# Routed experts in tiles of 128 tokens with the tokens stationary, in a pipeline of slots, instead of jobs of 256 rows

## The reference

```python
x = x + cross_attention(layernorm(x), ctx)       # 16 heads, causal mask
n = layernorm(x)                                 # 3584 x 512
probs = softmax(n @ gate_w.T)                    # 8 experts, the best 2 are taken
h1 = einsum("nc,efc->enf", n, expert_fc1)        # F_MOE = 352
h2 = einsum("nc,efc->enf", n, expert_fc2)
out_e = einsum("enf,ecf->enc", silu(h1) * h2, expert_proj)
y = einsum("ne,enc->nc", combine, out_e)         # combine: the 2 chosen probabilities
shared = (silu(n @ shared_fc1.T) * (n @ shared_fc2.T)) @ shared_proj.T   # F_SHARED = 1408
x = x + y + sigmoid(n @ shared_gate_w.T) * shared
```

## Time and profile before

| | us |
|---|---|
| median of 3 runs | 1603.74 |
| lowest and highest | 1602.83, 1603.98 |
| profiled execution, its own time | 1605.36 |
| its span, first to last instruction | 1603.6 |
| PE busy in the span | 1562.4 (97%) |
| DVE, ACT, POOL busy | 871.7 (54%), 633.1 (39%), 552.1 (34%) |

### The profile page before, as it was taken

The page is one execution under the profiler, slowest core; times in us unless marked ns, Lnnn a source line. Parts: engine busy times, 40 slices in busy tenths (PEclk is TensorE's granted clock), DMA queues, the critical chain, the costliest instruction groups (busy, mean ns, idle before and its releaser), DMA issues.

```text
span 1603.6 us, 32042 instructions
## 1 busy us (share of the span) xinstructions
PE 1562.4 (97%) x11388; PEld 1333.7 (83%) x11388; DVE 871.7 (54%) x1685; ACT 633.1 (39%) x1970; POOL 552.1 (34%) x507
## 2 busy tenths in 40 slices
PE   6999999999889999999999999999999999999998
PEld 5888888888678899999999999788788888888886
DVE  5667777776655666666666666554433232232322
ACT  5877777777823333333333333332112111121111
POOL 3233445544342365555555555121100101000010
PEclk9999999999999999999999999999999999999999
DMA  5133445443365366666666666354402103030110
GB/s 184 54 94 94 96 89 97 92 93 70 98 180 123 133 253 237 236 245 241 237 245 236 243 224 243 141 197 164 132 27 74 58 0 107 24 105 26 60 46 27
DMA packets 85684, 213.53 MB, mean 133 GB/s; under 512 B 38208, under 2 KB 39232, under 8 KB 80864
## 3 DMA queue, kind: packets, MB, share of 16 engines
q1 hardware_dynamic: 73424, 179.20, 34.7%
q0 software_dynamic: 12176, 33.20, 6.2%
HBM read 163.35 MB, written 49.02 MB: 132 GB/s over the span
## 4 chain that ended last, share of the span: by engine, by line
PE 89%; DVE 3%; issue 3%; ACT 2%; POOL 2%; DMA 1%; SPq 0%; DVEq 0%; POOLq 0%; ACTq 0%
PE psum L665 56%; PE psum L974 11%; PE psum L919 9%; PE psum L763 2%; PE psum L890 2%; PE psum L754 2%; PE psum L852 2%; ACT probs L1073 1%; PE psum L782 1%; PE psum L791 1%; PE psum L814 1%; PE psum L771 1%; POOL xn L1285 1%; DMA wj_raw<-in_wq 1%; PE psum L678 1%
## 5 line engine op out<-in xcount | busy, mean ns | idle before, releaser
L665 PE MATMUL psum<-gT_hi,wj_hi 128*128 128x256 f32 (+1 forms) x840 | 239.2, 285 | 0.0
L665 PE MATMUL psum<-gT_lo,wj_hi 128*128 128x256 f32 (+1 forms) x840 | 236.7, 282 | 0.0
L665 PE MATMUL psum<-gT_hi,wj_lo 128*128 128x256 f32 (+1 forms) x840 | 236.0, 281 | 0.0
L1360 POOL DMA_INDIRECT routed<-expert_out_dram,slot_b x56 | 56.2, 1004 | 487.6 <-DVE slot_b L1757 335.6
L665 PE MATMUL psum<-nT_hi,ws_hi 128*128 128x512 f32 x528 | 209.5, 397 | 6.1 <-DVE nT_lo L1709 6.1
L1775 DVE TENSOR_TENSOR h_s<-psum,silu_s 128x512 f32<-128x512 f32 x66 | 45.6, 691 | 306.2 <-PE psum L665 306.2
L665 PE MATMUL psum<-nT_hi,ws_lo 128*128 128x512 f32 x528 | 210.7, 399 | 0.0
L665 PE MATMUL psum<-nT_lo,ws_hi 128*128 128x512 f32 x528 | 210.0, 398 | 0.0
L1322 POOL TENSOR_SCALAR wj_hi<-wj_raw 128x2816 fp32r<-128x2816 f32 x68 | 136.5, 2024 | 151.9 <-PE psum L919 128.9
L1073 ACT ACTIVATE probs<-psum,minus_max 112x112 f32<-112x112 f32 x512 | 176.2, 429 | 2.5 <-DVE minus_max L1455 2.5
L1699 DVE TENSOR_TENSOR wj_lo<-wj_raw,wj_hi 128x2816 fp32r<-128x2816 f32 x70 | 169.2, 2417 | 0.8 <-ACT wj_hi L1165 0.7
(11 more groups left out here) (219 smaller groups left out, 3578.4 us busy)
## 6 DMA issues: line engine op xcount, KB each, us to landing
wj_raw<-in_w_experts SPq DMA_DIRECT2D x35, 2176.0 KB, 8.4
expert_out_dram<-y_c SPq DMA_DIRECT2D x35, 512.0 KB, 2.7
wj_raw<-in_w_shared SPq DMA_DIRECT2D x22, 768.0 KB, 5.6
base<-x_dram SPq DMA_DIRECT2D x8, 1024.0 KB, 5.9
x_in<-in_x SPq DMA_DIRECT2D x32, 224.0 KB, 4.5
x_res<-in_x SPq DMA_DIRECT2D x32, 224.0 KB, 3.9
x_dram<-x SPq DMA_DIRECT2D x32, 224.0 KB, 3.0
normed_dram<-xn SPq DMA_DIRECT2D x32, 224.0 KB, 4.9
```

What stands on the lines that cost most here:

```text
L665: mm = pe.matmul(out_ap, u, v, start=(n == 0), stop=(n == last))
L1360: pool.indirect_dma_start(out=routed[:, b % 2, c, :], out_offset=None, in_=expert_out_dram, in_offset=bass.IndirectOffsetOnAxis(ap=slot_b[ ...
```

## The change

The expert stage works on 63 tiles of 128 token rows. The first 56 positions of the table hold 28 pairs (two tiles of one expert, one load of weights), the last 7 hold odd tiles of one expert each, with a load of their own. They are worked in 7 rounds of 9: four pairs and then one odd tile. So there are 35 weight loads as before.

Tokens are now stationary also in the hidden products: 128 tokens x 128 channels stay, and all 352 features of one matrix move. h1, h2 and h then have tokens on the partitions, so h must be transposed before the projection (`rows_up`: 3 transposes, at columns 0, 128 and 224; the weight rows of the overlapping 32 features are zero in the third block). The projection has 3 x 3 products of 512 columns for a tile.

Each engine runs slots: PE in slot k does the hidden products of tile k, the transposes of h of k-1, the transposes of the tokens of k+2, the projection of k-2. There is one PSUM bank for each of h1, h2, hT, xT and y, one `h_c`, three buffers of xg, gT, hT and y_c, and three of the weights (pairs alternate between two, odd tiles have the third). Weights are loaded and split in two parts (`fc` 2816 columns, `pj` 1536) with semaphores of their own, spread over the slots by `splits`. ACT alone empties y. The first tile's weights are no longer loaded ahead with expert 0 fixed, but after the table, which is worked out across 128 partitions and brought to one row by two products on PE. In the last round the first shared chunk and the first tokens of the third stage are split in slots 8 and 7.

The table, the order of the weight splits, and the first weights' load:

```diff
-        NJOBS = (2 * NTOK + EXPERTS * (JOB - 1)) // JOB
+        TILES = (2 * NTOK + EXPERTS * (P - 1)) // P
+        ROUNDS = TILES // ROUND
+        PAIRS, SINGLES = 4 * ROUNDS, ROUNDS
...
+        def splits(q, k, fc, pj):
+            if k == 0:
+                fc(q, 1)
+            elif k == 1:
+                pj(q, 0)
...
+            elif k == 3:
+                pj(q, 1)
+                pj(q, 4)
...
                 if g == NG and j == 2:
-                    wait_emptied(sp, NG, 1, "proj")
-                    sp.dma_start(wj_raws[0][:, :], w_experts[0]).then_inc(wjraw_loaded[0], 16)
...
+            sp.wait_ge(S["table_ready"], 1)
+            wait_emptied(sp, NG, 1, "proj")
+            load_fc(0, 0)
+            load_pj(0, 0)
```

PE, beside the last shared chunks, and in the stage:

```diff
             for c in TAIL_CHUNKS:
-                chunk0(c)
+                hidden0(c)
+                if c == TAIL_CHUNKS[0]:
+                    pe.wait_ge(S["table_step"], TABLE_STEPS - 1)
+                    for i in range(2):
+                        mm = pe.matmul(psum[0:1, 6, i * TILES:(i + 1) * TILES], tile_cols[0:TILES, i:i + 1], ident[0:TILES, 0:TILES], start=True, stop=True)
+                    mm.then_inc(S["table_step"], 1)
+                project0(c - 1)
...
+            def hidden(q, k):
+                w, b = weights_of(k), k % 3
+                if first_of(k):
+                    pe.wait_ge(S["wc_split"], fc_nth(q, 4 if k == 8 else k // 2))
+                pe.wait_ge(S["gT_split"], tile(q, k) + 1)
+                for half, (to, emptied_h, made) in enumerate(((H1_BANK, "silu_made", "h1_done"), (H2_BANK, "h_made", "h2_done"))):
...
+                    for c in range(KC):
+                        cols = slice((half * KC + c) * FE, (half * KC + c + 1) * FE)
+                        pairs.append(((gT_hi[b][:, c, :], gT_lo[b][:, c, :]), (wj_hi[w][:, cols], wj_lo[w][:, cols])))
+                    product(bank(to, P, FE), pairs).then_inc(S[made], 1)
+            def rows_up(q, k):
+                pe.wait_ge(S["h_made"], tile(q, k) + 1)
...
+                for i, at in enumerate(F_AT):
+                    mm = pe.transpose(psum[:, HT_BANK, i * P:(i + 1) * P], h_c[:, at:at + P], ident[:, :])
...
+            def slot(q, k):
+                if is_tile(q, k):
+                    hidden(q, k)
+                if is_tile(q, k - 1):
+                    rows_up(q, k - 1)
+                if is_tile(q, k + 2):
+                    tokens(q, k + 2)
+                if is_tile(q, k - 2):
+                    project(q, k - 2)
```

ACT's slot, and what it does before the last shared chunk:

```diff
+            def slot(q, k):
+                if is_tile(q, k - 3):
+                    y_out(q, k - 3)
+                if is_tile(q, k):
+                    silu_of(q, k)
+                if is_tile(q, k - 1):
+                    rows_hi(q, k - 1)
+                if is_tile(q, k + 2):
+                    tokens_hi(q, k + 2)
+                if is_round(q, ROUNDS - 1):
+                    if k == 7:
+                        split_nT_hi(1)
+                    if k == 8:
+                        split_ws_hi(0)
...
+            for c in TAIL_CHUNKS:
+                if c == SC - 1:
+                    act.wait_ge(w_fc_loaded[0], 16)
+                    act.activation(wj_hi[0][:, FC_COLS], wj_raws[0][:, FC_COLS], ACT.Copy).then_inc(S["wc_hi_made"], 1)
                 chunk0(c)
```

DVE's product of silu(h1) and h2:

```diff
+            def h_of(q, k):
+                if not (isinstance(q, int) and tile(q, k) == 0):
+                    dve.wait_ge(S["hT_done"], tile(q, k))
+                dve.wait_ge(S["silu_made"], tile(q, k) + 1)
+                dve.wait_ge(S["h2_done"], tile(q, k) + 1)
+                dve.tensor_tensor(h_c[:, :], bank(H2_BANK, P, FE), silu_c[:, :], ALU.mult).then_inc(S["h_made"], 1)
```

More of the change, by code:

```diff
@@ L184, in build_program @@
         chosen = sa("chosen", [SEQ, TB + 1, EXPERTS])
[L185 to L190, removed]
+        tile_no_i, tile_no = sa("tile_no_i", [P, 2], I32), sa("tile_no", [P, 2])
+        expert_no, expert_at = sa("expert_no", [P, EXPERTS]), sa("expert_at", [P, EXPERTS])
+        steps_f = sa("steps_f", [P, EXPERTS, 2, STEPS])
+        over = sa("over", [P, EXPERTS, 2, STEPS])
+        counts, ends = sa("counts", [P, EXPERTS, 2]), sa("ends", [P, EXPERTS, 2])
+        jb = {n: sa("jb_" + n, [P, EXPERTS]) for n in
+              ("total", "begin", "begin2", "end2", "at", "late", "odd_at", "from_pair", "from_odd", "pair", "odd", "tile")}
+        spilled = sa("spilled", [P, 1])
+        tile_cols = sa("tile_cols", [P, 2])
         v_sb = sa("v_sb", [SEQ, 2, C])
@@ L342, in jobs @@
-        def jobs(eng, body):
-            pairs = (NJOBS - 2 - 3) // 2
-            for n in range(3):
-                body(n, n % 2)
-            with eng.Fori(0, pairs) as i:
-                body(2 * i + 3, 1)
-                body(2 * i + 4, 0)
-            for n in range(3 + 2 * pairs, NJOBS):
-                body(n, n % 2)
-        def last_job(n):
-            return isinstance(n, int) and n == NJOBS - 1
-        def is_job(n):
-            return not isinstance(n, int) or n < NJOBS
-        def times(k, n, p):
-            return (k // 2) * (n - p) + k
@@ L625, in _, with body @@
+            def body(q):
+                for k in range(ROUND):
+                    slot(q, k)
+            rounds(sp, body)
+            for k in range(ROUND, ROUND + 3):
+                store_y(ROUNDS - 1, k - 3)
+            for b in range(3):
+                sp.wait_ge(y_stored[b], 16 * TILES // 3)
             sp.wait_ge(S["phase_c_done"], 4)
@@ L893, in hidden @@
-            def hidden(n, p, i):
-                at, rows = F_CHUNKS[i]
-                for c, stage in enumerate(("h1", "h2")):
-                    b = take_c(n, stage, i)
-                    pairs = []
-                    for k in range(KC):
-                        cols = slice(c * KC * FE + k * FE + at, c * KC * FE + k * FE + at + rows)
-                        pairs.append(((wj_hi[p][:, cols], wj_lo[p][:, cols]), (gT_hi[:, k, :], gT_lo[:, k, :])))
-                    product(bank(b, rows, JOB), pairs).then_inc(filled_c[b], 1)
@@ L940, in _ @@
             pe.wait_ge(h2_emptied, SC)
-            tokens(0, 0, range(KC))
+            tokens(0, 0)
             project0(SC - 1)
-            jobs(pe, job_body)
-            pe.wait_ge(S["y_filled"], NJOBS)
+            tokens(0, 1)
+            rounds(pe, body)
+            for k in range(ROUND, ROUND + 2):
+                slot(ROUNDS - 1, k)
+            pe.wait_ge(S["y_done"], TILES)
             pe.sem_inc(S["phase_c_done"], 1)
@@ L1132, in split_ws_hi, with y_out @@
+            def y_out(q, k):
+                b, nth = turn(q, k)
+                if not (isinstance(q, int) and tile(q, k) < 3):
+                    act.wait_ge(y_stored[b], 16 * (nth - 1))
+                act.wait_ge(S["y_done"], tile(q, k) + 1)
+                act.activation(y_c[b][:, :], bank(Y_BANK), ACT.Copy).then_inc(S["y_emptied"], 1)
             def split_ws_hi(i):
@@ L1171, in _ @@
-            act.wait_ge(S["y_emptied"], JT * NJOBS)
+            for k in range(-2, 0):
+                slot(0, k)
+            rounds(act, body)
+            for k in range(ROUND, ROUND + 3):
+                slot(ROUNDS - 1, k)
+            act.wait_ge(S["y_emptied"], TILES)
             act.sem_inc(S["phase_c_done"], 1)
```

652 lines of the change are left out of this document (372 added, 280 removed).

## The result

The changed kernel takes 1554.62 us (median of 4, 1553.38 to 1559.25), the one before 1603.86 beside it: ratio 0.9692 [0.9663, 0.9721]. The time lies in the range of 1534 to 1566 and 10.6 us above the predicted 1544, and outside the 1538 to 1550 that the prediction gave for its own account of the change. Timed again at the end of the study, with the kernel before at 1604.82, it took 1554.57.

A forecast was written before the change was run, and what follows sets the result against it. PE, busy 97% of the span, was taken to bound the kernel. -54.5 + 0.3 - 5.3 = -59.5 from the profiled 1605.36 us gave 1545.9, about 1544 as a median; range 1534 to 1566, own account 1538 to 1550.

The forecast's parts named there:

- The start: From the table to the first expert tiles: a wait gone, two PE products, later ids and gather; +0.3 us, -0.4 + 0.2 + 0.5.
- The stage: Expert stage: 63 tiles of 6.79 us on PE, 427.8 us against 482.3; -54.5 us.
- the 352-column matmul: Hidden products: 164 ns each, on a line between 256 and 512 columns (columns / 2.4 GHz + 17); own range 160 to 167.
- Rival B: Hidden products: leftover per matmul shrinks at 352 columns; 157.5 ns, 10 us less, 1534 us (1518 without any leftover); 8%.
- The slot's cover: Expert slots: other engines' work fits beside PE's 6.79 us, long splits having 1.3 us to spare; 0 us.
- Rival A: Expert slots: a gather or split comes late in some; mean 0.1 to 0.45 us in 63 slots, 1550 to 1572 us; 22%.
- Rivals C: Hidden products: moving weights cost as 512 columns, 232 ns; slot 8.42 us, stage 530.6, total 1647 us; 5%.
- the transposes' effect on the clock: Expert stage: transposes might not count as busy for the clock; 0.77 in 6.79 us against 0.88 in 13.78; moved no chance.
- Rival D: Start: ids behind weights, PE out of work 2.7 us, clock down after (+1.8); 1548 us, inside the own range, no separate chance.
- a split begins only after POOL's: Expert slots: DVE's low-part split follows POOL's high-part split, each pair's first part at least one slot before PE asks; cost 0.
- The end: Passage to the shared stage: early splits remove 3.55 us idle, 1.76 clock loss and 0.18 wait, drain adds 0.2; -5.3 us.
- the 1.76 of clock behind it: First 48 shared matmuls: 12.96 us under a fallen clock instead of twice 5.60; -1.76 us, part of the end's -5.3.

The follow-up runs named there:

- x5: Changed kernel with hidden products of 256 moving columns in place of 352, features 256 to 351 left out; 1503.49 us (one run).
- x1: Changed kernel with the first tile's weights loaded ahead of the table again, expert 0 fixed; 1549.58 us.
- x2: Changed kernel with ids of tiles 4 to 6 issued earlier (4, 5 before the third buffer's loads, 6 before the base store), that buffer's first split a slot later; 1549.11 us.
- x3: Changed kernel with the edits of x1 and x2 together; 1548.95 us.
- x6: Changed kernel with the weights' high parts made by ACT instead of POOL, in the same slots; 1549.71 us.
- x8: Changed kernel with the edits of x1, x2 and x6, and y in three PSUM banks in turn instead of one; 1547.69 us.
- x4: Changed kernel with the first shared weights and third-stage tokens split only after the last tile's h, as before the change; 1555.75 us.
- x10: Changed kernel, unedited, timed again at the end of the study; 1554.57 us, ratio 0.9685 to the kernel before.
- x9: x8 with ids of tiles 3 to 5 also ahead of the second load into the first weight buffer (hidden part); 1545.99 us, ratio 0.9651 to the kernel before.

## Why the prediction came out as it did

The direction was right, and so was the mechanism of the gain: PE's stream alone sets the slot. The start was not: it was put at +0.3 and cost 11.6 us more. That the time still came within 10.6 us of the forecast is in part luck, since the mis-sized matmul gave back 5.7.

- *The stage* (-54.5 forecast): right in kind, PE alone sets the slot. 63 slots of 6.70 are 422.1 us, -60.2. The term mis-sized is the 352-column matmul: 160 ns, the low end of my own range, for 164. I drew one line through two points with the same leftover; x5 shows that with tokens stationary the leftover at 256 is 11, not 17, so the point at 256 came from a stream that doesn't exist any more. Rival B had the direction (its 157.5 is 2.5 ns off, my 164 is 4), for another reason: it took the 11 from a stationary operand of 96 columns, and here all 128 are loaded.
- *The slot's cover* (0 forecast): right in the steady part, with no idle time at all in 56 slots. Rival A (a gather or a split late in some slots; ids behind 1.4 MB loads as its reason) named what happened at the start, and the time fell in its 1550 to 1572; what it had wrong is the place, since the waits are in the first slots alone. Rivals C (a slot of 8.42 us) and the transposes' effect on the clock did not happen: 1.00. (For the clock at 548.7 the prediction names a group of rows that begins at 552.5; the trace has 1.00 from 544 to 550 too.)
- *The start* (+0.3 forecast): wrong by 11.6 us, the largest error. PE idled 9.3 us from 553 to 597, and the fallen clock took 0.2 * 0.66 + 0.5 * 3.76 + 0.2 * 4.00 = 2.8 us behind the long wait. Rival D had the mechanism (ids behind weights, then the clock down) with a price of 2.7 + 1.8. Two steps failed. First, I followed only the first tile's ids. The first tiles' gathers cost 2.0 us, a loss of the size that I had bounded; the ids of tile 4, behind two weight loads and a store, cost 3.46 in one wait (x1, x2). SP and POOL are in order with three buffers, so one late load moves those behind it: here also POOL's copy of the projection's weights, and so the subtraction that PE waited for next. Second, "a split begins only after POOL's" took the durations as independent of each other: beside POOL's copy (576.03 to 578.57) a subtraction of 1.75 us took 4.08 at 576.11, and PE waited 1.98 (x3, x6). The first gather was held up by 2.7 us by a subtraction, more than the 1.49 that PE waited for its rows; no run separates this from the late ids. The gathers' mean of 1.88 us in the earlier trace rows already held such waits (the shortest is 0.95), the subtractions' 2.42 held none.
- *The end* (-5.3 forecast): idle time of 3.55 became 0.29, and 12.96 became 11.32. What I left out is y's single bank in the drain: without hidden products between two projections PE waits twice for ACT (1.4 us), and x8 takes both waits away. So -3.6 came; x4 puts 3.35 us on the splits' new place, give or take 0.7.
- *Chance*: the first stage ended at 525.66 in this profile. In the ten profiles of x1 to x10, with nearly the same code up to there, it did at 517.6 to 523.7. So this one profile came out late.

For the stretch the forecast was -57.7 (without the 1.76 of clock behind it), measured -49.7, so 8.0 off: -5.7 (width) + 11.6 (start: 12.1 for 0.5) + 1.5 (end) = 7.4. The 0.6 us left is within the 0.7 by which two profiles of one kernel differ.

Where the start's loss sits is shown (x1, x2, x3, x6, x9), and that both causes take part. How much each is worth alone can't be told to better than a microsecond, since the gains overlap. Also the medians fell more than the stretches in x1 (5.0 against 2.4), x2 (5.5 against 2.8) and x6 (4.9 against 3.2). The kernel before, timed beside each, stayed within 1603.3 to 1604.8, so the chips don't explain it, and the cause stays open.

## What to carry to other kernels

Where a pipeline is filled in a steady loop, work out the fill apart, and for as many tiles as there are buffers and two more: which small load stands behind which large one on an in-order queue. Before a small load is written behind a large one, ask whether it could go first. And when a change puts a subtraction on DVE beside a copy on POOL that never ran beside it, its time from the old trace isn't enough: ask what it costs when the two exclude each other. Last, look at the clock behind a wait as well as at the wait: a stretch that ends with the wait leaves that part of the price out.

## What the runs showed of the hardware

- DVE's subtraction of two SBUF tensors and POOL's copy exclude each other: in x3 1.75 us became up to 6.13 and 3.09 became 4.34. With the copy on ACT that is gone (x6: 1748 to 1786 ns over 35).
- DVE's subtraction also holds up the issue of POOL's indirect DMA (0.95 us became 3.65), but not the other way round: 64 subtractions of the kernel before ran beside such an issue at 1.75 and 3.08 to 3.09 us.
- ACT makes the same high part no slower than POOL: 2554 ns for 2816 columns on average, POOL 2718, its waits for DVE included (median 2566).
- Behind 6 us in which PE worked 0.81 us the granted clock was 0.50 from 580.2 to 585.6; behind a single wait of 3.2 us in x9 it was 0.85, 0.50 and 0.76 over 5.6 us, which cost 1.7 us.
- With the tokens stationary and a weight load for each matmul, one costs 118 ns at 256 columns (x5), 160 at 352 and 232 at 512.
- A load of 0.5 KB issued 3 to 4 us behind two of 2.2 MB together landed 7.2 us after its issue (540.03 to 547.23); behind two such loads and a store of 1 MB it took 9.5 (from 562.95).
